# Second MLP product in token order, with per-token statistics, in a fused tower block on one core

## The reference

```python
h = tok(x)                                    # einsum over the inputs: 16 x 512 x 256
x = layernorm(h)
x = x + attention(ln(x, g1, beta1)) @ wo      # causal linear attention
h2 = ln(x, g2, beta2)
x = x + gelu(h2 @ w1 + b1) @ w2 + b2          # 256 -> 1024 -> 256
h = h + x
xn = layernorm(h)                             # over the 256 features of each token
logits = xn @ gate_w.T                        # 8 routed experts and a shared one
y  = shared(xn) * gw[:, 8]                    # silu(xn @ g) * (xn @ u) @ d, 512 wide
y += sum over chosen experts e of global_w[:, e] * expert_e(xn)   # up to 4, capacity 1280
out = h + y
```

## Time and profile before

| | us |
|---|---|
| median of 3 runs | 2729.38 (2725.92 to 2731.68) |
| the profiled execution's own time | 2748.85 |
| its span | 2747.1 |
| TensorE busy | 2405.4 (88%), x22832 |
| TensorE weight loads | 1738.9 (63%) |
| VectorE busy | 1892.2 (69%) |
| GpSimd busy | 1566.7 (57%) |
| ScalarE busy | 1462.3 (53%) |

### The profile page before, as it was taken

One profiled execution on the slowest core, in us unless ns is written; L12 is line 12 of the kernel. 1 busy time (PEld: TensorE's weight loads), 2 busy tenths in 40 slices (PEclk: granted clock), 3 DMA queues, 4 the chain that ended last, 5 costly groups with the idle time before them and its releaser, 6 DMA issues. The chain is left out here.

```text
span 2747.1 us, 61186 instructions
## 1 busy us (share of the span) xinstructions
PE 2405.4 (88%) x22832; PEld 1738.9 (63%) x22832; DVE 1892.2 (69%) x4174; ACT 1462.3 (53%) x2731; POOL 1566.7 (57%) x1546
## 2 busy tenths in 40 slices
PE   4799999999999999999999858898888898986564
PEld 3588788888888888888887724444444444443453
DVE  2577777777777777777777736787777777865342
ACT  3466666666666666666666534434443444432232
POOL 1465656565665656565656522665566556655576
PEclk8999999999999999999999979999999999998887
DMA  4111111111121111111110020121121111100675
GB/s 146 43 61 63 41 60 61 60 44 60 60 64 40 44 40 44 36 48 36 44 40 13 10 98 24 64 72 51 47 69 67 50 41 49 36 20 9 143 137 79
DMA packets 115060, 152.21 MB, mean 55 GB/s; under 512 B 16537, under 2 KB 75917, under 8 KB 114768
## 3 DMA queue, kind: packets, MB, share of 16 engines
q1 hardware_dynamic: 88880, 124.46, 14.1%
q0 software_dynamic: 23808, 21.74, 4.5%
q10 hardware_dynamic: 2080, 2.10, 0.2%
HBM read 81.71 MB, written 90.96 MB: 63 GB/s over the span
## 5 line engine op out<-in xcount | busy, mean ns | idle before, releaser
L952 POOL TENSOR_TENSOR qkl<-fz,qkh 128x512 f16<-128x512 f32 x256 | 307.6, 1201 | 309.5 <-DVE qkh L849 305.2
L1817 POOL DMA_INDIRECT slot_dram<-xt,slot_u x256 | 257.6, 1006 | 74.6 <-issue 73.6
L521 PE MATMUL pF<-nh,qk_h 128*128 128x256 f16 x1024 | 282.0, 275 | 8.1 <-DVE nl L836 4.4
L522 PE MATMUL pF<-nh,qk_l 128*128 128x256 f16 x1024 | 281.2, 275 | 0.0
L523 PE MATMUL pF<-nl,qk_h 128*128 128x256 f16 x1024 | 281.2, 275 | 0.0
L964 POOL TENSOR_TENSOR ol<-on,oh 128x256 f16<-128x256 f32 x256 | 171.8, 671 | 153.5 <-ACT oh L786 153.5
L971 POOL TENSOR_TENSOR kvl<-kvacc,kvh 128x260 f16<-128x260 f32 x192 | 150.2, 782 | 107.8 <-ACT kvh L794 107.8
L1797 POOL TENSOR_TENSOR al<-az,ah 128x512 f16<-128x512 f32 x64 | 79.2, 1238 | 220.9 <-DVE ah L1586 220.9
L763 ACT ACTIVATE sh<-sm 128x512 f16<-128x512 f32 x256 | 159.3, 622 | 84.6 <-DVE sm L872 84.6
L846 DVE SCALAR_TENSOR_TENSOR fz<-pF,ez 128x512 f32<-128x512 f32 x256 | 175.3, 685 | 31.9 <-ACT ez L746 29.8
L740 ACT ACTIVATE rz<-pF 128x512 f32<-128x512 f32 x256 | 150.7, 589 | 86.0 <-PE pF L523 81.4
(11 more groups left out here) (313 smaller groups left out, 8577.0 us busy)
## 6 DMA issues: line engine op xcount, KB each, us to landing
xs<-in_x SPq DMA_DIRECT2D x128, 256.0 KB, 2.6
slot_dram<-blank SPq DMA_DIRECT2D x8, 1360.0 KB, 6.0
xg<-slot_dram SPq DMA_DIRECT2D x40, 272.0 KB, 3.2
h_dram<-hT SPq DMA_DIRECT2D x32, 256.0 KB, 2.1
x_dram<-x SPq DMA_DIRECT2D x32, 256.0 KB, 2.1
at_dram<-at SPq DMA_DIRECT2D x32, 256.0 KB, 2.2
x0b<-x_dram SPq DMA_DIRECT2D x16, 512.0 KB
atb<-at_dram SPq DMA_DIRECT2D x16, 512.0 KB
```

Source lines behind the costliest of these rows:

```text
L521: pe.matmul(out, wh, mh, start=first, stop=False, skip_group_check=True)
L522: pe.matmul(out, wl, mh, start=False, stop=False, skip_group_check=True)
L952: nc.gpsimd.tensor_tensor(qkl[:, pair:pair + 2, cols], fz[:, n % 2, :, :], qkh[:, pair:pair + 2, cols], ALU.subtract).then_inc(fl_ready, 1)
L1817: nc.gpsimd.indirect_dma_start(io["slot_dram"], bass.IndirectOffsetOnAxis(slot_u[:, c, k:k + 1], 0), xt[:, i % 2, c, :], None, bounds_chec ...
```

## The change

The second product of the MLP swaps its operands: 128 tokens of `gh` or `gl` are the stationary side and 256 columns of `w2` the moving one, so `pY` comes out in token order. The residual is added in the same banks before it, by eight fp32 matmuls of `hx` with 64 times the identity (`ident_w`). ScalarE copies `pY` to `ht` in two halves; VectorE takes mean and variance of each token by `bn_stats` and `bn_aggr`, so ScalarE's logarithm and exponential work on 128x4 elements, and `xn` is made chunk by chunk. `mean3`, `var3`, `hp`, `xc3`, `sq3` and `turn_sums` go. High and low parts are written straight into `xt` (now three deep); TensorE transposes them back to feature order in a bank of their own, `pX`, and ScalarE copies them to `xf`, from which `gate_up` and `logits` read. The token counts go to columns of `pL`, beside the logits. ScalarE casts `gh`; VectorE runs three links of the routing per group of `w1`, and all of links 31 to 51 (`rest`) after the last `gate_up`. `down` is cut in three pieces between the two halves of `turn_rows` and the `logits`.

```diff
@@ constants, tiles
+XT = 3
+COUNTS = 64
...
-        hp = sb("hp", [DT, T])
-        xc3, sq3, ln3, rs3, xn = sb("xc3", [DT, T]), sb("sq3", [DT, T]), sb("ln3", [T]), sb("rs3", [T]), sb("xn", [DT, T])
-        xnh, xnl = sb("xnh", [DT, T], F16), sb("xnl", [DT, T], F16)
-        xt = sb("xt", [2, CH, ROW], U32)
-        ht = sb("ht", [CH, D])
+        ht = sb("ht", [2, CH, D])
+        st3, mv3 = sb("st3", [CH, 6]), sb("mv3", [CH, 2])
+        ln3, rs3, xn = sb("ln3", [CH]), sb("rs3", [CH]), sb("xn", [CH, D])
+        xt = sb("xt", [XT, CH, ROW], U32)
+        xf = sb("xf2", [2, DT, T], F16)
+        xnh, xnl = xf[:, 0, :, :], xf[:, 1, :, :]
...
+        pX = bank("pX")
@@ order of the steps, body
                 s["w2"](i, range(7, FT))
+                s["sums3"](i)
...
+                s["rstd3"](i)
                 if before:
                     s["gate_up"](i - 1, after, (0,))
-                s["mean3"](i, before)
...
                 if before:
-                    s["gate_up"](i - 1, after, (1, 2))
-                s["var3"](i)
+                    s["gate_up"](i - 1, after, (1,))
+                s["norm3"](i)
+                if before:
+                    s["gate_up"](i - 1, after, (2,))
+                s["low3"](i, 0)
+                s["low3"](i, 1)
                 if before:
                     s["gate_up"](i - 1, after, (3,))
-                s["rstd3"](i)
+                    s["rest"](i - 1)
+                s["rows_ahead"](i)
+                s["turn_rows"](i, 0)
                 if before:
-                    s["down"](i - 1)
-                s["turn_rows"](i, before)
+                    s["exp2"](i - 1)
+                    s["down"](i - 1, (0, 1))
+                s["turn_rows"](i, 1)
+                if before:
+                    s["down"](i - 1, (2,))
                 s["logits"](i)
-                s["turn_sums"](i)
+                if before:
+                    s["down"](i - 1, (3,))
@@ TensorE
             def w2(i, js):
...
+                    for c in range(CH):
+                        toks = slice(c * P, (c + 1) * P)
+                        for t in range(DT):
+                            at = c // 2 * D + t * P
+                            mm = pe.matmul(pY[c % 2][:, at:at + P], hx[:, t, toks], ident_w[:, :], start=c < 2 and t == 0,
+                                           stop=False, skip_group_check=True)
+                    mm.then_inc(hx_added, 1)
...
-                    for m in range(DT):
-                        cols = slice(m * P, (m + 1) * P)
-                        mm = three(pY[m][:, :], w2_h[:, j, cols], w2_l[:, j, cols], gh[:, j, :], gl[:, j, :],
-                                   j == 0, j == FT - 1)
+                    for c in range(CH):
+                        toks = slice(c * P, (c + 1) * P)
+                        mm = three(pY[c % 2][:, c // 2 * D:(c // 2 + 1) * D], gh[:, j, toks], gl[:, j, toks],
+                                   w2_h[:, j, :], w2_l[:, j, :], False, j == FT - 1)
...
+            def turn_rows(i, half):
+                pe.wait_ge(xnh_ready, count(i, 2, half + 1))
+                pe.wait_ge(xnl_ready, count(i, 2, half + 1))
+                if i > 0 or half > 0:
+                    pe.wait_ge(xf_ready, count(i, 2, half))
...
+                            mm = pe.transpose(bank16[:, w * P:(w + 1) * P],
+                                              xt[:, i % XT, 2 * half + c, words].bitcast(F16), ident16[:, :])
@@ ScalarE
             def centre2(i):
+                exp_ln_tables(nc, act)
...
+                    act.wait_ge(gz_ready, count(i, FT, j + 1))
+                    if j == 0 and not at_start(i):
+                        act.wait_ge(w2_done, count(i, 1, 0))
+                    nc.scalar.activation(gh[:, j, :], gz[:, j % 4, :], ACT.Copy).then_inc(gh_ready, 1)
+
+            def sums3(i):
+                act.wait_ge(w2_done, count(i, 1, 1))
...
+                for b in range(2):
+                    nc.scalar.activation(ht[:, i % 2, b:CH:2, :], pY[b][:, :].rearrange("p (c n) -> p c n", c=2), ACT.Copy,
+                                         scale=1 / W2_SCALE).then_inc(ht_ready, 1)
...
+            def norm3(i):
...
+                for half in range(2):
+                    act.wait_ge(xn_ready, count(i, CH, 2 * half + 2))
+                    nc.scalar.activation(xt[:, i % XT, 2 * half:2 * half + 2, 0:D // 2].bitcast(F16),
+                                         xn[:, 2 * half:2 * half + 2, :], ACT.Copy).then_inc(xnh_ready, 1)
...
+            def turn_rows(i, half):
+                act.wait_ge(xt_done, count(i, 2, half + 1))
...
+                nc.scalar.activation(xf[:, :, :, half * 2 * P:(half + 1) * 2 * P].rearrange("p a t n -> p (a t) n"),
+                                     pX[:, :].bitcast(F16).rearrange("p (w n) -> p w n", n=2 * P),
+                                     ACT.Copy).then_inc(xf_ready, 1)
@@ VectorE
-                    ve.wait_ge(gz_ready, count(i, FT, j + 1))
-                    nc.vector.tensor_copy(gh[:, j, :], gz[:, j % 4, :]).then_inc(gh_ready, 1)
...
-                        routing(i - 1, EXP1_AFTER + 2 * j, EXP1_AFTER + 2 * j + 2)
+                        routing(i - 1, EXP1_AFTER + 3 * j, EXP1_AFTER + 3 * j + 3)
...
+            def sums3(i):
...
+                for b in range(2):
+                    ve.wait_ge(ht_ready, count(i, 2, b + 1))
+                    for c in (b, b + 2):
+                        nc.vector.bn_stats(st3[:, c, :], ht[:, i % 2, c, :]).then_inc(st3_ready, 1)
+                    for n, c in enumerate((b, b + 2)):
+                        ve.wait_ge(st3_ready, count(i, CH, 2 * b + n + 1))
+                        nc.vector.bn_aggr(mv3[:, c, :], st3[:, c, :]).then_inc(mv3_ready, 1)
+
+            def norm3(i):
...
+                for c in range(CH):
+                    nc.vector.tensor_scalar(xn[:, c, :], ht[:, i % 2, c, :], mv3[:, c, 0:1], rs3[:, c:c + 1],
+                                            ALU.subtract, ALU.mult).then_inc(xn_ready, 1)
@@ GpSimd
+            def low3(i, half):
+                gp.wait_ge(xnh_ready, count(i, 2, half + 1))
...
+                nc.gpsimd.tensor_tensor(rows_[:, :, D // 2:D].bitcast(F16), xn[:, 2 * half:2 * half + 2, :],
+                                        rows_[:, :, 0:D // 2].bitcast(F16), ALU.subtract).then_inc(xnl_ready, 1)
+
+            def rows_ahead(i):
+                if i < SEQS - 1:
+                    sums(i + 1)
+                if i < SEQS - 2:
                     rows(i + 2)
@@ constants of the routing
-ROUTE_CUTS = (43, 46, 49, ROUTE_STEPS)
+COUNTED_AFTER = 30
```

More of the change, by code:

```diff
@@ L1207, in run @@
             s["counts"](SEQS - 1)
+            s["exp2"](SEQS - 1)
+            s["rest"](SEQS - 1)
             s["gate_up"](SEQS - 1, None, range(ST))
-            s["down"](SEQS - 1)
+            s["down"](SEQS - 1, range(ST))
         def at_start(i):
@@ L1325, in gate_up, with down @@
                         mm.then_inc(gu_done, 1)
[L1327 to L1336 removed]
+            def down(i, ks):
+                pe.wait_ge(ht_ready, 2 * SEQS if i == SEQS - 1 else count(i + 1, 2, 2))
+                for k in ks:
                     pe.wait_ge(ah_ready, count(i, ST, k + 1))
@@ L1399, in counts, with nothing @@
                 mm.then_inc(cum_done, 1)
-            def nothing(i):
+            def nothing(i, *rest):
                 pass
-            run(pe, dict(mean2=mean2, var2=var2, w1=w1, w2=w2, mean3=mean3, gate_up=gate_up, var3=var3, down=down,
-                         centre2=nothing, scale2=nothing, shift2=nothing, mask=nothing,
-                         rstd3=nothing, logits=logits, turn_rows=turn_rows, turn_sums=turn_sums,
-                         counts=counts))
+            run(pe, dict(mean2=mean2, var2=var2, w1=w1, w2=w2, gate_up=gate_up, down=down,
+                         centre2=nothing, scale2=nothing, shift2=nothing, mask=nothing, sums3=nothing,
+                         rstd3=nothing, norm3=nothing, low3=nothing, rows_ahead=nothing, logits=logits,
+                         rest=nothing, exp2=nothing, turn_rows=turn_rows, counts=counts))
         @block.scalar
@@ L1506, in nothing @@
                 pass
-            run(act, dict(mean2=mean2, centre2=centre2, var2=var2, scale2=nothing, shift2=shift2, mask=nothing, w1=w1, w2=nothing, mean3=mean3, gate_up=gate_up, var3=nothing,
-                          rstd3=rstd3, down=nothing, logits=logits, turn_rows=turn_rows, turn_sums=turn_sums,
-                          counts=counts))
+            run(act, dict(mean2=mean2, centre2=centre2, var2=var2, scale2=nothing, shift2=shift2, mask=nothing, w1=w1,
+                          w2=nothing, sums3=sums3, rstd3=rstd3, norm3=norm3, low3=low3, rows_ahead=nothing,
+                          gate_up=gate_up, down=nothing, logits=logits, turn_rows=turn_rows, counts=nothing,
+                          rest=nothing, exp2=exp2))
             act.wait_ge(ew.w_in[0], 16)
@@ L1856, in mean2 @@
```

(6 more changed lines are left out.)

247 lines of the change are left out of this document (100 added, 147 removed).

## The result

The changed kernel takes **2734.22 us** as the median of 17 runs (2728.64 to 2747.16), for 2729.38 of the kernel before in 17 runs beside them (2722.29 to 2738.18). The ratio is 1.0023 with an interval of 1.0012 to 1.0034: slower by the 0.2% that a measurement of this kernel can tell. The forecast was 2663 with a range of 2620 to 2705, and it was wrong by 71 us.

The account below looks back on a forecast made before the run. TensorE was taken to set the pace. A sequence sums to 16.7 + 8.3 + 25.0 + 0.8 = 50.8 us for 54.65; 54 + 5.3 - 2.0 + 9.4 = 66.7 less gives 2663, range 2620 to 2705.

Parts of the forecast that it names:

- TensorE's work: TensorE, per sequence: 2.2 us less work, 43.9 in all, with w2 at 0.109 a matmul and the residual 2.0.
- The rival in which the weight loads bind: Second product: loads of 0.10 us not hidden behind its 96 matmuls, 154 us on top, 2817; 4% with other slowdowns.
- The mask's gap and its clock: Ahead of the token counts: 2.6 us of gap and 1.4 of clock go, mask ready some 4 us ahead.
- The gap ahead of the transposes: Behind gate_up: first transposes wait until 16.7 us after T, a gap of 4.6 where 1.83 stood.
- From the transposes to w1: Transposes, down and logits: 0.9 + 5.2 + 0.75 = 6.9 us, with the clock's 1.4 making 8.3.
- The rest: From w1 through mean2, residual and w2 to the counts: 25.0 us, plus 0.8 of wait in w1.
- The wait in w1: Fifth gelu waits for the first gl behind six scatters: 0 to 1.6 us too late, taken as 0.8.
- The range: Whole kernel: 2620 to 2705 us at 79%, from unknowns of -2.2 to +2.6 us per sequence.
- The first sequence: Sequence without a shared expert beside it: 39.2 us for 44.5, 5.3 less, but T(0) 2.0 later.
- The end: Last scatters on GpSimd: those of sequence 14 start at about 21 and land at 43.6, 9.4 us less.
- the routed phase: Phase of the kernel that was forecast not to change.
- The rival that names locks at each small step: VectorE and GpSimd locks lengthen the gap ahead of the transposes, 3.9 us more per sequence, 2715 to 2730; 9%.

Follow-up runs that it names:

- a ring of eight: The changed kernel with gz eight deep instead of four, so no gelu waits for a gl of its own sequence: 2693.88 us, ratio 0.9861 to before.
- the kernel with the cuts back: The changed kernel with routing links 31 to 43 behind the counts again, the others between gate_up's groups, nothing in rest: 2709.14 us, ratio 0.9917.
- second execution: The kernel before run and traced once more with no edit: 2735.18 us, one execution.
- the fastest kernel: The changed kernel with hx, x1 and hb right behind the second product, xnl ahead of gate_up's third group, gz eight deep: 2636.68 us, ratio 0.9679.

## Why the prediction was wrong, point by point

- **TensorE's work.** Right. The first 84 matmuls of `w2` go from 2060.82 to the counts at 2069.99, 0.109 each as I took it, with new weights for each. The residual stands 1.8 us ahead of them (from 2059.03), for 2.0. The rival in which the weight loads bind (2817) fell on that spacing. With it fell the rule that the prediction took from the Trainium skill (TensorE: Matmul & The Clock Gate, the section on the mechanism of packing), that a load overlaps a running matmul only where its row group differs; the spacing by it, an estimate, would be some 0.21. The same section also says that a load into the background weight buffer is pulled ahead of running matmuls, and the 0.109 agrees with that.
- **The mask's gap and its clock.** Right: the gap is gone, `m` is ready at 2068.62 and the counts start at 2069.99. The margin is 1.4 to 5.3 us from step to step, where some 4 were forecast; with a ring of eight, where TensorE comes earlier, the counts wait 0.60 for it.
- **The gap ahead of the transposes.** Right: 16.93 us behind T for the 16.7 that were worked out, 4.61 of gap for 4.6. The steps of the walk hold as well: the four `xn` end 12.1 behind T for 11.8, the second cast of them 12.75 for 12.4. With GpSimd's `al` beside them the four took 2.22; in the kernel with the cuts back they took 1.38, 0.35 each, as they had been priced. In part this is luck: the two `n2l`, priced at 1.4 together, took 2.31 beside another `al`, and the steps ahead of them were 0.4 shorter than walked.
- **From the transposes to w1.** 9.40 for 8.3. Of the difference 0.82 is the wait of the logits for `xf`, for which the forecast had no term, though it named the exponential between the two copies. That exponential waits for the blocked links. What is left, 1.7 where 1.4 was taken, goes with the half clock.
- **The rest.** 27.29 for 25.0 + 0.8. Without the two gaps (2.09 and 0.16) it is 25.04.
- **The wait in w1**, the term "ends 0 to 1.6 us too late; I take 0.8", is the step that failed. It rested on "when rest is through (about 25 us after T)". It was through at 27.9, and the scatters began at 28.9: I had applied the lock once, to `xn`, and not to the six links and the cast that the change puts beside GpSimd's `xnl`, `al`, `hx` and `x1`, 6.7 us in all. The fifth gelu was 2.38 late, and TensorE had a gap of 2.09; in the longer steps a half clock behind it, for which there was no term, adds 1.7.
- **What it was worth.** From T(1) to T(15) a step takes 55.12 for 50.8, 4.3 more, 60.5 us in 14 steps. With a ring of eight, without this wait, a step takes 3.1 less, and the term was 0.8: so it was short by 2.3 of the 4.3. With `hx` and `x1` away from the links a step takes 3.3 less, since the logits' wait for `xf` goes as well. In the step from 2018.03 the three differences are 0.2 + 1.1 + 1.5 = 2.8, which is 53.6 for 50.8; most of the others carry the clock as well, the first two have a gap of 3.3 in `w1`, and one has the delayed scatters (59.07).
- **The range.** Its upper end has the same fault. The terms named for it, 1.1, 0.5, 0.8 and one more lock of 1.15, make 3.6 and not 2.6, that is 50 us and 2713; and 4.3 came.
- **The first sequence**: 40.75 for 39.2; T(0) stood 37.86 behind the statistics ahead of it, where the earlier trace rows belong to an execution with 37.03 and the other one had 38.76. The 2.0 us for the residual don't show.
- **The end.** 9.4 us less were forecast, 0.6 came: from T(15) (2457.53) to the end of the last scatter it takes 73.3, for 73.9 in the kernel before's second execution (and 79.3 in the first, of the earlier trace rows). 5.4 of the 9.4 were that execution's own. `slot_u` comes 47.1 behind T(15) for 43.6: the scatters started 23.0 behind it and not 21, and had one hole of 2.90.

```profile
2480.51 0.99 POOL L1843 DMA_INDIRECT slot_dram<-xt,slot_u  x1 [5.82 <-DVE slot_u L1753]
...
2485.69 0.98 POOL L1843 DMA_INDIRECT slot_dram<-xt,slot_u  x1 [2.90 <-issue]
...
2504.59 0.18 DVE L1753 SCALAR_TENSOR_TENSOR slot_u<-slot_f,far 128x16 uint32<-128x16 f32 x1 [6.13 <-DMA slot_dram<-xt,slot_u]
```

The sum can be drawn against the second execution of the kernel before, the nearer of the two to its median. In its terms, with the forecast in brackets: the steps 11.4 more (54 less), the first sequence 2.8 less (5.3 less), the end 0.6 less (9.4 less), the routed phase 0.5 more (nothing), and T(0) 10.6 earlier (2.0 later), which is the first phase of two single executions and no gain of the change. That is 2.1 less where 66.7 less were forecast, 64.6 of the miss; the steps alone are 65.4. The rest of the 71.2 lies in how far these two executions stand from their medians (5.8 above 2729.38 and 1.2 below 2734.22).

The rival that names locks at each small step (2715 to 2730) had the mechanism; it stood at 9%, and looked for it ahead of the transposes only. What stays open is why the half clock behind the gap of 2.09 comes in some steps and not in others: the two stretches above differ in the clock alone, and no run varied that gap's length by itself.

## What to carry to other kernels

When a change moves a chain of small VectorE operations, write down for each one which GpSimd operation runs beside it, and price it at that operation's length: the same chain costs 0.2 or 1.2 us a link (its `TENSOR_REDUCE` links excepted), and moving the neighbour was worth 43.5 us here, two thirds of what was forecast for the whole change. Follow each delay to the ring or queue that hands it to the bounding engine; four more places in a ring of tiles were worth 40 us without any work removed. A term read off one execution, its steps or its end, should be checked against a second execution before it goes into a sum.

## What the runs showed of the hardware

- A VectorE operation with a single input and 4 elements per partition waits for a GpSimd operation as well as a large one does: 1.17 us beside it, 0.17 alone. `bn_stats` (0.41) and `TENSOR_REDUCE` of 128x256 (0.42) take the same time inside a GpSimd operation as alone, and so does `az`, one input of which lies in PSUM (0.69).
- Behind the same gap of 2.09 us the granted clock was 0.60 over 4.3 us in one sequence and 1.00 over 2.5 in the next, which gives two step lengths, 53.6 and 55.3, in an otherwise identical loop.
- fp32 matmuls of 128 columns, new weights each, come as 16 records in 1.95 us for eight matmuls. `bn_stats` of 256 columns takes 0.41 us in the mean, `bn_aggr` 0.17, and four normalisations of 256 columns with a scale and a bias per partition 1.38 with nothing beside them.
- In the fastest kernel 12 of the 14 steps have no gap over 1.52 us, and the granted clock is 1.00 in them; in the other two, with gaps of 1.91 to 2.65, it is 0.97. In the changed kernel, with a gap of 4.61 in each, it is 0.88 to 0.97.
- One execution of the kernel before took 13.7 us more than another: 15.0 more in its 14 steps, 5.4 more in the phase's last 80 us, and 5.4 less up to T(0), with 1.3 less in the rest.
